# Moving the third PSUM bank from the maximum tiles to the score tiles in units 0 and 1 of a causal attention kernel

## What is computed

```python
x = _layernorm(x + _L0_attn_ref(x, W_Q, W_K, W_V, W_O))
x = _layernorm(x + _L0_ffn_ref(x, router_w, router_b, expert_w, expert_b))
# attention: softmax((Q K^T) / sqrt(32), causal) V, then W_O
# ffn: for each token the expert of the largest router probability, times that probability
```

## The kernel before, in words

| While | score tiles over | maximum tiles over |
|---|---|---|
| unit 0 | score0, score1 | maxp0, maxp1, proj1 (of unit 1) |
| unit 1 | score0, score1 | maxp0, maxp1, proj1 (of unit 2) |
| unit 2 | score0, score1, proj1 | maxp0, maxp1, proj0 (of unit 3) |
| unit 3 | score0, score1, maxp0, maxp1 | none |

## Time and profile before

### The profile page before, as it was taken

The page is one execution under the profiler, slowest core; times in us unless marked ns, Lnnn a source line. Parts: engine busy times, 40 slices in busy tenths (PEclk is TensorE's granted clock), DMA queues, the critical chain, the costliest instruction groups (busy, mean ns, idle before and its releaser), DMA issues. The chain is left out here.

```text
span 2493.7 us, 41857 instructions
## 1 busy us (share of the span) xinstructions
PE 2304.9 (92%) x14080; PEld 1479.0 (59%) x14081; DVE 1459.7 (59%) x3931; ACT 1030.1 (41%) x2105; POOL 872.5 (35%) x1535
## 2 busy tenths in 40 slices
PE   1999999999999999999999999999999999529998
PEld 1754575557554765467546754575547554318886
DVE  2576366735664476537664677366735664356665
ACT  2245424552446234633454245424552445133333
POOL 2323324332423243333232332324332422236665
PEclk9999999999999999999999999999999999759999
DMA  8632244313531353225321643144313530164443
GB/s 296 168 82 85 68 127 137 111 60 100 164 102 65 89 173 83 94 70 177 81 93 50 164 113 95 65 121 142 114 57 96 154 94 6 55 208 149 150 144 121
DMA packets 130936, 282.07 MB, mean 113 GB/s; under 512 B 33027, under 2 KB 42243, under 8 KB 128453
## 3 DMA queue, kind: packets, MB, share of 16 engines
q1 hardware_dynamic: 100920, 208.62, 28.1%
q0 software_dynamic: 28304, 70.64, 9.5%
q10 hardware_dynamic: 1536, 0.53, 0.1%
HBM read 133.04 MB, written 47.53 MB: 72 GB/s over the span
## 5 line engine op out<-in xcount | busy, mean ns | idle before, releaser
L704 ACT ACTIVATE probs<-score 128x512 f32<-128x512 f32 (+3 forms) x1216 | 563.5, 493 | 539.0 <-PE score L1044 517.7
L579 POOL TENSOR_SCALAR_AFFINE_SELECT probs<-probs 128x256 f32<-128x256 f32 x512 | 215.1, 424 | 703.8 <-ACT probs L704 700.7
L794 DVE CUSTOM_DVE_ANT_0 maxp<-maxp,mask_qk 128x384 f32<-128x384 f32 (+3 forms) x696 | 323.4, 506 | 210.1 <-PE maxp L1032 208.5
L1044 PE MATMUL score<-q_stack,k_stack 97*128 97x512 f32 (+2 forms) x1216 | 425.2, 372 | 21.5 <-ACT probs L704 20.0
L975 PE MATMUL proj<-xt,w_qk 128*128 128x512 f32 x1284 | 362.4, 399 | 52.2 <-DMA w_qk<-w_qk_parts 51.2
L1064 PE MATMUL y_ps<-probs,v 128*32 128x512 f32 (+3 forms) x3072 | 327.3, 498 | 12.5 <-DVE rows L819 12.3
L1032 PE MATMUL maxp<-k_stack,q_stack 96*128 96x512 f32 (+2 forms) x1024 | 329.2, 365 | 8.8 <-DVE tile_max L789 4.4
L1064 PE MATMUL den_ps<-probs,ones_f 128*32 128x512 f32 (+3 forms) x3072 | 319.0, 486 | 0.0
L1044 PEld LDWEIGHTS score<-q_stack,k_stack 97*128 97x128 f32 x1216 | 224.5, 189 | 136.0 <-ACT probs L704 89.9
L975 PEld LDWEIGHTS proj<-xt,w_qk 128*128 128x128 f32 x1284 | 238.6, 191 | 107.5 <-DMA w_qk<-w_qk_parts 49.9
L1032 PEld LDWEIGHTS maxp<-k_stack,q_stack 96*128 96x128 f32 x1024 | 180.5, 188 | 134.1 <-DVE tile_max L794 44.7
(11 more groups left out here) (163 smaller groups left out, 2932.6 us busy)
## 6 DMA issues: line engine op xcount, KB each, us to landing
w_qk<-w_qk_parts SPq DMA_DIRECT2D x64, 512.0 KB, 3.8
q_stack<-w_vo_parts SPq DMA_DIRECT2D x16, 2048.0 KB, 8.5
q_stack<-parts SPq DMA_DIRECT2D x512, 64.0 KB
k_stack<-parts SPq DMA_DIRECT2D x512, 64.0 KB
got<-dispatched SPq DMA_DIRECT2D x75, 257.0 KB, 2.7
xt_raw<-x_t SPq DMA_DIRECT2D x32, 512.0 KB, 9.2
q_stack<-parts POOLq DMA_DIRECT2D x256, 64.0 KB, 2.3
k_stack<-parts POOLq DMA_DIRECT2D x256, 64.0 KB, 2.3
```

The source lines that it names most:

```text
L579: nc.gpsimd.affine_select(out=block, in_=block, compare_op=ALU.is_ge, fill=0.0, base=0, pattern=[[0, 2], [1, P]], channel_multiplier=-1)\
L704: nc.scalar.activation(probs[:, 4 * (n % PROBS) + h, c:BANK], score_bank(u, 4 * j + h)[:, c:BANK], ACT.Exp, scale=SCALE).then_inc(exp_done ...
L794: top = nc.vector.tensor_tensor_reduce(out=tile, in0=tile, in1=mask_qk[:, BANK - cols:BANK], scale=1.0, scalar=-3.0e38, op0=ALU.add, op1=A ...
L1044: nc.tensor.matmul(score_bank(u, i)[:, c0:BANK], k_st[u % SETS][0:3 * DH + 1, h, kb * P:(kb + 1) * P], q_st[u % SETS][0:3 * DH + 1, h, t * ...
```

## The change

The rings of units 0 and 1 are made like that of unit 2: scores over score0, score1 and proj1, and the maxima of units 1 and 2 over maxp0 and maxp1. `score_passed` lets a score tile of these units start when the exponential three tiles back is done, where it was two. The wait for bank proj1 to be free of value job 7 moves from the third maximum tile of unit 1 to the third score tile of unit 0. No matmul, exponential or reduction is added, removed or put elsewhere in an engine's order.

```diff
         def max_ring(u):
 
-            return maxp + score if u == 0 else maxp + proj[1:2] if u < UNITS - 1 else maxp + proj[0:1]
+            return maxp + score if u == 0 else maxp if u < UNITS - 1 else maxp + proj[0:1]
 
         def score_bank(u, i):
 
-            ring = score + maxp if u == UNITS - 1 else score + proj[1:2] if u == UNITS - 2 else score
+            ring = score + (maxp if u == UNITS - 1 else proj[1:2])
             return ring[i % len(ring)]
 
         def score_passed(u, i):
 
-            if u < UNITS - 2:
-                return max(STILES * u + i - 1, 0)
-            return STILES * u + (max(i - 2, min(i - 1, 0)) if u == UNITS - 2 else max(i - 3, min(i - 2, -1)))
+            if u < UNITS - 1:
+                return max(STILES * u + i - 2, 0)
+            return STILES * u + max(i - 3, min(i - 2, -1))
...
                     if u == 0 and len(maxp) <= i < len(max_ring(u)):
                         pe.wait_ge(proj_free[i].sem, proj_free[i].at(b, 0))
-                    if u == 1 and i == len(maxp):
-                        wait_job(pe, b, proj_free, ("v", ROWT - 1))
...
                     c0 = min(c, BANK - 256)
+                    if u == 0 and i == len(score):
+                        wait_job(pe, b, proj_free, ("v", ROWT - 1))
                     pe.wait_ge(exp_done.sem, exp_done.at(b, score_passed(u, i)))
```

## The result

The changed kernel takes 2542.3 us (median of 4 runs, 2539.21 to 2544.57) against 2505.84 for the kernel before (2503.9 to 2508.15): a ratio of 1.0145, 95% interval 1.0129 to 1.0162. That is 36.5 us slower, where 38 were forecast.

The account below looks back on a forecast made before the run. PE was taken to bound the kernel. Maxima losses less score gains gave +4.1 - 1.67 = +2.4 us in unit 0 and +3.7 - 1.34 = +2.35 in unit 1, +38 over eight batches: 2544 us, range 2524 to 2564.

Parts of the forecast that it names:

- The bound: Units 0 and 1: PE sets the pace, busy 92% of the span, no other engine over 59%.
- the reading of the maxima: Maximum tiles: two banks' cost comes from when DVE finished the tile two places before; 4.1 us in unit 0, 3.7 in unit 1.
- The walk's thirteen places: Tile-by-tile count, delays carried on: seven late maximum tiles in unit 0, six in unit 1, together 7.8 us a batch.
- The gain of the third score bank: Score tiles at unit 0's start and both units' ends wait less: 1.67 us in unit 0, 1.34 in unit 1.
- The sum: Net loss of 2.4 us in unit 0 and 2.35 in unit 1, +38 us over eight batches, 2544 on the median.
- What was said of the rows: PE's waits: before score tiles from 20.0 to under 8 us, for DVE before maximum tiles from 6.9 to 25 or more.
- The Trainium skill's reading: Repeating gaps before score tiles on PE mean too few buffers: bank to the scores, up to 20.0 us faster, about 2486.
- The scores win: Rival: the thirteen places cost only 2.3 us a batch, all real score waits go; -20 us, 2486; chance 4%.
- a wash: Rival: new waits at the maxima merge to 3 us a batch; 2505 us; chance 3%.
- DVE falls behind for good: Rival: late tiles push DVE's copies and divisions, `weigh` waits too, full static lateness is paid; 2583 us; chance 8%.
- The clock: Rival: granted clock falls to 1.2 GHz in one unit, +48 us on top, 2590 us; chance 1%.

Follow-up runs that it names:

- the lent bank: Against the kernel before, proj1 goes to scores where no maximum tiles are at work and to maxima in between: 2486.22 us against 2509.94, ratio 0.9911.
- its other two profiles: Two repeats of the kernel before, unchanged, run for further profiles: 2509.68 and 2511.38 us.
- the second one of the changed kernel: A repeat of the changed kernel, unchanged, run for a further profile: 2548.28 us.
- all idle banks lent: Against the kernel before, scores have all five banks where no maximum tiles are at work, unit 2's last groups included: 2469.8 us, ratio 0.9839.
- both on two banks: Against the kernel before, scores of units 0 and 1 stay on two banks, maxima of units 1 and 2 also get two: 2574.85 us, ratio 1.0268.

## Why the prediction was right

**The bound, and the reading of the maxima.** Right. The wait rows before (20.0 against 6.9 us) spoke for the change; the count of how late each maximum tile would be with two banks spoke against it, and decided. The walk's thirteen places are the places where the changed kernel waits, seven in unit 0 and six in unit 1 (at one of them the tile behind the named one is the one that waits), and its sizes hold: alone, the missing bank costs unit 1 3.75 us (3.7 forecast) and batch 0's unit 0 4.3 (4.1).

**The gain of the third score bank.** Right: 1.34 us forecast for unit 1 and 1.3 measured with the lent bank; 24 us over the whole kernel, and 24 measured. In the lending kernel's profile unit 0 of batch 0 gained 1.4 of the 1.67 forecast (50.1 to 48.7). In the changed kernel the first maximum tile in unit 1 waits for the negated maxima as said: 6.1 us in eight batches, where it was 1.1 in four.

**The sum.** Unit 1: 54.6 us forecast, 54.5 to 54.6 measured in seven batches (56.1 in the eighth, in which the clock fell for a moment; this makes the average 54.7). Unit 0: 52.4 forecast, which batch 0 shows, and 53.6 on average. This isn't a cost of the change: unit 0 of the kernel before is itself at 51.6 in its other two profiles, so the change costs it 2.0 us there, 0.4 less than forecast; in batch 0 it costs the 2.4, and what makes the other batches cheaper isn't shown. (2.0 + 2.35) x 8 = 35 us, against 36.5 measured. The sum was right. Putting it on the median and not only on the profile was right, though I gave no reason for it: I had not asked why the recorded profile lay 10 us under the median.

**What was said of the rows.** The scores' waits were to fall under 8 us and fell to 8.4 with those on `proj`; those of the maxima were to rise to 25 or more and rose to 55.3, twice as much: the idle column gives nearly the whole of a wait over 0.4 us, and I had thought of more of it as hidden behind overlapping matmuls.

**The rivals.** The Trainium skill's reading (Perfetto Trace Analysis, Optimization Strategy: the same gap repeating on the busiest engine can mean too few buffers) was right of the place, since a bank there is worth 24 us. The 2486 that I made of it for this change left out what the bank costs where it is taken. "The scores win" and "a wash" are refuted. "DVE falls behind for good" too: PE's wait for DVE's copies of y fell from 12.3 to 10.1 us.

**The clock** came in, but small. In unit 1 of batch 5 of the changed kernel the granted clock falls to 0.50, that is 1.2 GHz, for 3.4 us, shortly after PE had stood idle for 1.38 us at the hand-over from unit 0 (a row of the timeline, then stretches with columns as in the earlier trace rows):

```profile
1503.79 0.66 PE L1030 MATMUL maxp<-k_stack,q_stack 96*128 96x256 f32 x4 [1.38 <-DMA q_stack<-neg_max]
...
1500.00:1505.00 5.00, 3.49 (x27) 2.05 (x27) 0.52 (x5) 1.60 (x8) 1.22 (x3) 1.00 0.03 7
1505.24:1508.65 3.41, 3.41 (x22) 1.56 (x20) 1.22 (x8) 0.78 (x2) 0.41 (x1) 0.50 0.00 0
```

That unit lasts 56.1 us where the others last 54.5 to 54.6, so one such fall costs 1.5 us, not the 48 of the rival. The three profiles of the kernel before have none inside units 0 to 3, and the second one of the changed kernel has none there either, so the falls don't make the loss. PE stands idle for 0.9 us or more 20 and 28 times in the attention part of the changed kernel's two profiles, against 2 to 4 times before, and only one and two falls follow: most waits of this length leave the clock at 1.00.

## What to carry to other kernels

Before a buffer is moved from one ring to another, don't compare the waits that both show today: count, tile by tile, how late each would start if its ring were one shorter, from the reader's ends in the trace, and carry the delay on within a run of tiles. A ring that shows no waits may be the one that needs its last buffer most, here because DVE takes 0.68 us for what PE delivers every 0.23 to 0.6 where tiles stand close. And look at when each side needs it: lent by phase, the same bank gave 24 us where moving it cost 36, and all idle banks lent gave 41.

## What the runs showed of the hardware

One stretch of a fixed program, with fixed data, varied from execution to execution by up to 2.6 us (batch 4 of the kernel before: 50.1, 51.3 and 52.7 us), while units 1 to 3 repeated within 0.1: unit 0 of batches 1 to 7. In it GpSimd scatters the previous batch's rows, and the DMA share is 0.53 (0.46 in batch 0's unit 0, 0.32 in unit 1). In batch 0, where there is nothing to scatter, unit 0 is the same in each profile of a kernel to 0.2 us. What differs is how soon a reader follows its tile. In batch 0 of every profile, and in all batches of the recorded profile of the kernel before, ACT starts some 0.32 us after PE starts a 256-column score tile of groups 2 and 3. In batches 1 to 7 of each of the two later profiles of the kernel before, 26 exponentials of groups 2 to 4 start over 0.25 us later behind their tile than in the recorded one (0.6 to 1.2 us behind it in all), two to five in a batch; in those of the changed kernel 8 do in each, and in three of the fourteen batches none. DVE is late at such places too. So it isn't made by the change. It makes most of unit 0's 51.6 in place of 50.3 us: in batch 3 of the second profile PE loses 0.58, 0.45 and 0.70 us behind such readers in groups 3 and 4. A later wait for the negated maxima adds to it in some batches (1.30 us in batch 4 of the third). In batch 3 of the changed kernel the exponential of the tile at 922.43 starts 0.75 us after it:

```profile
922.43 0.28 PE L1044 MATMUL score<-q_stack,k_stack 97*128 97x256 f32 x1
...
923.18 0.38 ACT L704 ACTIVATE probs<-score 128x256 f32<-128x256 f32 x1 [1.97 <-PE proj L1044]
```

The DMA traffic is one candidate, by its place; but its amount alone doesn't decide, since around the start of batch 3's unit 0 the DMA share is 0.87 in the recorded profile, which has no late start, and 0.86 in the changed kernel's, which has. That the instructions reach ACT and DVE late is another. Neither was tested: the scatters can't be moved out of unit 0 without `rows` being overwritten, and leaving them out wasn't tried.

Short falls of the granted clock to 0.50 stand in the attention part of ten of the thirteen profiles, one to three in each, and at different places in repeats of a kernel. Shortly before each of them PE had stood idle for 0.9 to 2.1 us. A unit that holds one is longer than its fellows: with both on two banks, unit 0 lasts 57.7 and 57.6 us in batches 1 and 3, which hold a fall, and 54.7 to 55.0 in batches 4 to 7, which hold none.
